# A fused RWKV-style block on Trainium2: two pairs of mixes packed four wide on TensorE, with a new order of the step and PSUM banks from a table

## The reference

```python
xn = _ln(x, ln1_w, ln1_b)
sx = _token_shift(xn, state[:, i1])
xxx = jnp.tanh((xn + sx * maa_x) @ maa_w1).reshape(b, l, 5, 1, EXTRA_MAA)      # 5 x 32
xxx = jnp.matmul(xxx, maa_w2).reshape(b, l, 5, E)                              # five mixes, each 32 -> 512
x5 = xn[:, :, None] + sx[:, :, None] * (maa_stack + xxx)
w = jnp.exp(-jnp.exp(time_decay + jnp.tanh(x5[:, :, 1] @ decay_w1) @ decay_w2))
r = x5[:, :, 3] @ Wr.T;  k = x5[:, :, 0] @ Wk.T;  v = x5[:, :, 2] @ Wv.T       # by heads
g = jax.nn.silu(x5[:, :, 4] @ Wg.T)
def step(s, rkvw):
    a = k_t[:, :, :, None] * v_t[:, :, None, :]
    out = jnp.einsum('bhk,bhkd->bhd', r_t, u * a + s)
    return (a + w_t[:, :, :, None] * s, out)
att = group_norm_over_heads(outs) * gn_w + gn_b
x = x + att * g @ Wo.T
xn2 = _ln(x, ln2_w, ln2_b);  sx2 = _token_shift(xn2, state[:, i0])
rr = jax.nn.sigmoid((xn2 + sx2 * ffn_maa_r) @ ffn_Wr.T)
kk = jnp.square(jax.nn.relu((xn2 + sx2 * ffn_maa_k) @ ffn_Wk.T))
return x + rr * (kk @ ffn_Wv.T)
```

## Time and profile before

| | |
|---|---|
| median of 3 runs | 1659.32 us (1658.87 to 1660.46) |
| the profiled execution | 1657.67 us, its span 1655.9 us |
| TensorE matmul busy | 1590.0 us, 96% of the span, 19990 records |
| VectorE busy | 997.2 us, 60% |
| ScalarE busy | 513.0 us, 31% |
| GpSimd busy | 624.3 us, 38% |
| DMA, mean | 41 GB/s; SyncE's queue 12.2% of 16 engines |
| mean granted TensorE clock | 0.989 |

### The profile page before, as it was taken

How to read it: one execution, slowest core, us unless ns; L and a number is a source line. 1 busy time by engine, 2 the same in 40 slices (tenths; PEclk the granted TensorE clock), 3 DMA queues, 4 the chain that set the end, 5 groups by cost and what they waited for, 6 DMA issues and landing times.

```text
span 1655.9 us, 46091 instructions
## 1 busy us (share of the span) xinstructions
PE 1590.0 (96%) x19990; PEld 1200.0 (72%) x19990; DVE 997.2 (60%) x1990; ACT 513.0 (31%) x910; POOL 624.3 (38%) x512
## 2 busy tenths in 40 slices
PE   8989799999999999999999999999999999999988
PEld 7877577777767777776777777677776767777554
DVE  3263765667666566756657675665767557564642
ACT  1123222323232232423233232323333233332331
POOL 3242532535243253524425252442525235252411
PEclk9999799999999999999999999999999999999999
DMA  7010101102010110201001010110101011010200
GB/s 276 1 37 25 50 23 35 48 7 64 22 62 22 34 50 7 65 22 61 23 21 51 18 64 22 45 39 20 50 20 62 24 35 48 9 49 21 69 11 25
DMA packets 56425, 67.73 MB, mean 41 GB/s; under 512 B 23264, under 2 KB 40032, under 8 KB 55200
## 3 DMA queue, kind: packets, MB, share of 16 engines
q1 hardware_dynamic: 56224, 64.79, 12.2%
HBM read 43.75 MB, written 8.39 MB: 31 GB/s over the span
## 4 chain that ended last, share of the span: by engine, by line
PE 78%; DVE 14%; ACT 4%; POOL 2%; issue 2%; SPq 0%; DMA 0%; ACTq 0%; POOLq 0%; DVEq 0%
PE pair L1116 28%; PE pair L1124 19%; PE pair L1170 4%; PE at_ps L1050 4%; PE at_ps L1043 3%; PE pair L1194 2%; PE kv_ps L1072 2%; DVE kT L590 2%; PE att_ps L1107 2%; PE pair L1132 2%; PE pair L1196 2%; DVE x L679 2%; POOL cen L482 2%; PE pair L1150 2%; DVE gT L709 1%
## 5 line engine op out<-in xcount | busy, mean ns | idle before, releaser
L1116 PE MATMUL pair<-x,wts 128*128 128x256 f32 x2048 | 459.1, 382 | 14.7 <-ACT kT L864 14.3
L1116 PEld LDWEIGHTS pair<-x,wts 128*128 128x128 f32 x2048 | 383.8, 190 | 76.2 <-ACT kT L864 17.0
L456 POOL TENSOR_TENSOR x<-x,xnT 128x1024 f32<-128x1024 f32 x80 | 178.6, 2233 | 218.1 <-DVE x L679 217.4
L679 DVE SCALAR_TENSOR_TENSOR x<-pair,vecs,sx 128x256 f32<-128x256 f32 x320 | 132.4, 475 | 117.1 <-PE pair L1170 116.7
L873 ACT ACTIVATE at<-at_ps 128x512 f32<-128x512 f32 x128 | 76.3, 596 | 184.1 <-PE at_ps L1050 183.9
L1124 PE MATMUL pair<-wts,cen 128*128 128x512 f32 x240 | 110.8, 604 | 0.0
L1050 PE MATMUL at_ps<-rm,kc 128*16 128x128 f32 (+1 forms) x2048 | 110.8, 276 | 0.0
L1124 PE MATMUL pair<-wts,yT 128*128 128x512 f32 x240 | 109.6, 599 | 0.3 <-POOL yT L494 0.3
L1116 PE MATMUL pair<-yT,wts 128*128 128x256 f32 x480 | 107.8, 382 | 0.0
L1124 PE MATMUL pair<-wts,sx 128*128 128x512 f32 x240 | 107.0, 599 | 0.7 <-ACT cen L859 0.7
L1116 PEld LDWEIGHTS pair<-yT,wts 128*128 128x128 f32 x480 | 89.9, 190 | 14.4 <-issue 2.8
(11 more groups left out here) (194 smaller groups left out, 2760.2 us busy)
## 6 DMA issues: line engine op xcount, KB each, us to landing
rm<-rst SPq DMA_DIRECT2D x1024, 12.0 KB
xu<-in_x SPq DMA_DIRECT2D x16, 512.0 KB, 3.7
wts<-in_wts SPq DMA_DIRECT2D x8, 1024.0 KB, 14.6
kvs<-in_s SPq DMA_DIRECT2D x32, 256.0 KB, 3.3
s<-in_s SPq DMA_DIRECT2D x32, 256.0 KB, 2.9
x<-in_x SPq DMA_DIRECT2D x15, 512.0 KB
out<-sx SPq DMA_DIRECT2D x15, 512.0 KB, 3.6
prev<-in_prev SPq DMA_DIRECT2D x32, 4.0 KB, 3.2
```

What stands on the lines that cost most here:

```text
L456: gp.tensor_tensor(t, t, xnT[:, :, :, 1:L1].rearrange("p g b t -> p (g b) t"), ALU.add).then_inc(x5_ready, 1)
L679: last = ve.scalar_tensor_tensor(seqs(x5[q], g), ps[:, :, g * L:(g + 1) * L], vecs[:, vec, g:g + 1], seqs(sx, g), ALU.add, ALU.mult)
L1116: last = pe.matmul(ps[:, g // 2, TB * (g % 2):TB * (g % 2 + 1)], wts[:, m, k, g * P:(g + 1) * P], source[:, k, :], start=(k == 0), stop=(k ...
```

## The change

The mixes are done in three goes. **mixWV** does the mixes W and V together, and **mixKR** K and R: for each channel group and sequence the products of the two mixes follow each other, so that four products in a row lie on four different groups of 32 rows and go to four different PSUM banks. mixG stays alone. The order of the step is rewritten on every engine but SyncE: v is computed first, its two halves around z and decay, then mixKR, k, mixG, r, and g last, behind wo. c02_1 and c1v_1 of the running block move ahead of z. Banks come from a table (`BANK`, and `BANK_FIRST` for step -1) instead of the parity, and `x5_ready` counts in the order V, W, K, R, G. Step -1 gets lists of its own (the `-1` entry of `PE_EDGE` and its like), and `IDLE` is rewritten.

```diff
-MIXES = {"mixW": (MW, 1, 0, 0), "mixK": (MK, 0, 1, 1), "mixG": (MG, 2, 0, 2),
-         "mixR": (MR, 3, 1, 3), "mixV": (MV, 2, 0, 4)}
+MIXES = {"mixV": (MV, 2, 1, 0), "mixW": (MW, 1, 0, 1), "mixK": (MK, 0, 0, 2), "mixR": (MR, 3, 1, 3),
+         "mixG": (MG, 2, 0, 4)}
+JOINT = {"mixWV": ("mixW", "mixV"), "mixKR": ("mixK", "mixR")}
-DENSE = {"k": (WK, 1, 1), "g": (WG, 0, 2), "r": (WR, 1, 3), "v": (WV, 0, 4)}
+DENSE = {"k": (WK, 0, 2), "g": (WG, 0, 4), "r": (WR, 1, 3), "v": (WV, 1, 0)}
...
+BANK = {"mixW": 0, "mixV": 1, "wv": 1, "c02_1": 0, "c1v_1": 1, "z": 0, "v": 1, "decay": 0, "mixK": 0, "mixR": 1,
+        "yT": 0, "k": 1, "mixG": 0, "r": 1, "wo": 0, "g": 1, "x2T": 0, "xT": 1, "c02_0": 0, "kk": 1, "c1v_0": 0,
+        "rr": 1, "h": 0}
+TASKS = list(BANK)
...
-DVE_ORDER = ["mixW", "kv0", "attb1", "chain1", "gn_sum", "wv", "gn_var", "mixK", "c02_1", "gn_rec", "mixG",
+DVE_ORDER = ["mixV", "kv0", "attb1", "mixW", "chain1", "gn_sum", "wv", "c02_1", "c1v_1", "gn_var", "chain1b", "gn_rec",
...
+DVE_EDGE = {-1: ["mixV", "mixW", "mixK", "mixR", "ln1_stats", "ln1", "mixG", "chain0", "xT", "c02_0", "chain0b",
+                 "c1v_0", "g"],
...
+            def joint_mix(names, i, at_):
+
+                a = at_.plus(1)
+                for name in names:
+                    for semaphore, value in readers_before(name, i, at_):
+                        pe.wait_ge(semaphore, value)
+                if i == -1 and names[0] == "mixW":
+                    pe.wait_ge(lora_in, 16 * 8)
+                pe.wait_ge(h_ready, a.count(1, 1))
+                for g in range(G):
+                    for b in range(NB):
+                        for name in names:
+                            lo = MAA * ((MIXES[name][1] + 2 * b) % 4)
+                            last = pe.matmul(bank(name, i)[:, b, g * L:(g + 1) * L],
+                                             maa2[b][lo:lo + MAA, g * P:(g + 1) * P],
+                                             h1[lo:lo + MAA, b * L:(b + 1) * L], start=True, stop=True)
+                            if g == G - 1 and b == NB - 1:
+                                last.then_inc(done[name], 1)
```

More of the change, by code:

```diff
@@ L74 @@
         "ln2", "x2T", "kk", "rr", "wv")
-PE_LAST = {LAST: ["kt0", "V7", "kv0", "wv.0", "aT1", "A0", "wv.1", "V0", "A1", "c02_1", "V1", "c1v_1", "A2", "V2",
+PE_EDGE = {-1: ["mixWV", "v.0", "z", "v.1", "mixKR", "decay", "k.0", "k.1", "mixG", "r.0", "r.1", "xT", "c02_0", "g.0",
+                "g.1", "h", "c1v_0"],
+           LAST: ["kt0", "V7", "kv0", "wv.0", "aT1", "A0", "wv.1", "V0", "A1", "c02_1", "V1", "c1v_1", "A2", "V2",
                   "yT", "A3", "V3", "kt1", "wo.0", "kv1", "wo.1", "aT0", "A4", "V4", "yT@0", "A5", "V5", "x2T", "A6", "V6",
@@ L82 @@
             LAST + 1: ["x2T@1", "kk@1", "rr@1"]}
-DVE_LAST = {LAST: ["kv0", "attb1", "chain1", "gn_sum", "wv", "gn_var", "c02_1", "gn_rec", "c1v_1", "chain1b",
+DVE_EDGE = {-1: ["mixV", "mixW", "mixK", "mixR", "ln1_stats", "ln1", "mixG", "chain0", "xT", "c02_0", "chain0b",
+                 "c1v_0", "g"],
+            LAST: ["kv0", "attb1", "chain1", "gn_sum", "wv", "gn_var", "c02_1", "gn_rec", "c1v_1", "chain1b",
                    "attb0", "kv1", "gn_sum@0", "gn_var@0", "gn_rec@0", "wo", "ln2_stats", "ln2", "x2T", "wo@0",
@@ L86 @@
             LAST + 1: ["wo@1", "ln2_stats@1", "ln2@1", "wv", "x2T@1", "wv@0", "wv@1"]}
-POOL_LAST = {LAST: ["gn_sub", "rch1", "wv", "c02_1", "gn_scale", "bon1", "yT", "rch1b", "gn_sub@0", "gn_scale@0",
+POOL_EDGE = {-1: ["mixV", "mixW", "mixK", "mixR", "ln1_stats", "mixG", "rch0", "c02_0", "rch0b", "bon0"],
+             LAST: ["gn_sub", "rch1", "wv", "c02_1", "gn_scale", "bon1", "yT", "rch1b", "gn_sub@0", "gn_scale@0",
                     "ln2_stats", "yT@0", "ln2_stats@0", "gn_sub@1", "gn_scale@1", "yT@1"],
@@ L91 @@
            LAST + 1: ["out", "out@0", "out@1"]}
-IDLE = {(-2, "xT"): 14, (-2, "h"): 27, (-1, "mixW"): 3, (-1, "z"): 17, (-1, "mixG"): 6, (-1, "k.0"): 3, (-1, "g.0"): 4,
-        (-1, "mixR"): 10, (-1, "mixV"): 6, (-1, "r.0"): 4, (-1, "v.0"): 4, (-1, "c1v_0"): 5, (-1, "h"): 12, (0, "mixW"): 3,
-        (0, "kt0"): 5, (0, "A0"): 14, (0, "V0"): 18}
+IDLE = {(-2, "xT"): 14, (-2, "h"): 27, (-1, "mixWV"): 3, (-1, "v.0"): 14, (-1, "mixKR"): 4, (-1, "decay"): 6,
+        (-1, "k.0"): 4, (-1, "c02_0"): 10, (-1, "c1v_0"): 2, (0, "mixWV"): 2, (0, "kv0"): 2, (0, "A0"): 12}
 class Block:
@@ L830, in step @@
             def step(i, at_):
[L831 removed]
+                for name in DVE_EDGE.get(i, DVE_ORDER if i < LAST else []):
                     if "@" in name:
@@ L1156, in stage @@
                                              ut[:, k, b * L:(b + 1) * L], start=(k == 0), stop=(k == G - 1))
-                elif name in MIXES:
-                    m = MIXES[name][1]
-                    if i == -1 and name == "mixW":
-                        pe.wait_ge(lora_in, 16 * 8)
+                elif name == "mixG":
                     pe.wait_ge(h_ready, a.count(1, 1))
```

56 lines of the change are left out of this document (30 added, 26 removed), and 3 rows, old and new, of the table PE_ORDER.

## The result

The changed kernel takes **1645.24 us** (median of 4 runs, 1644.55 to 1647.49), and the kernel before, run beside it on the same chip, 1659.09 (1658.65 to 1660.46). The ratio is 0.9917, 95% interval 0.99 to 0.9935: faster, by 13.9 us. 1631 was forecast. The time lies inside the range of 1619 to 1652, but the gain is half of the one worked out, 13.9 instead of 28.3 us, so half of the sum needs explaining.

What follows compares the result with a forecast made beforehand. TensorE's own work bounds full steps, a cross-engine chain the start. -1.10 us over thirteen steps (-14.3) and -14.0 at the start give -28.3 on 1657.67, so 1629.4; median 1631, range 1619 to 1652.

Steps and rivals of the forecast that it cites:

- The mixes: TensorE's two joint mixes a step: 32 records at 34 ns take 1.09 us instead of 2.18, so -2.18 us a step.
- The first and second rival: Joint mixes: first, packing under fourfold, 1.4 us each, 1641 (0.22); second, four groups no faster than two, 2.18, 1666 (0.08).
- Waits that go: TensorE's three recurring full-step waits, before g (0.98), mixR (0.34) and c02_1 (0.30), vanish: -1.62 us a step.
- V next to A: V products directly behind their A wait for ScalarE's copy: V1, V2, V3, V6 take 1.15 us, V0 0.87; +0.92 a step.
- New waits: TensorE waits in full steps before k.0 (0.73), xT (0.7) and rr.0 (0.35): +1.78 us a step.
- Covered, I think: Other full-step places, among them kv0, wv, chain1, yT, wo, x2T, c02_0 and h, were expected to bring no new wait.
- The third rival: VectorE, behind a late chain1b, reaches mixK late, so k.0 starts 1.2 us later: +16, 1647 us; chance 0.10.
- The start: Up to step 1: chain0b 14.9 us earlier, V0 at 91, then about 67 us to the next mix; -14.0 us.
- the fourth rival: The start gains only half, because the clock falls or a weight load holds v: 1638 us; chance 0.10.
- Steps 15, 16: 0: The last two steps were forecast to neither gain nor lose time.
- its own two terms of 7: Low end of the range: joints at 0.87 us (-7) and one of the three new waits not coming (-7).

Runs made afterwards that it cites:

- The run with mixW first: Changed kernel with mixW ahead of kv0 and attb1 in VectorE's order: 1638.90 us, ratio 0.9876.
- the run with dummies: Changed kernel with dummy products added on TensorE, 16 before V0 and 7 before k.0 of step 0, 28 before V0 of step 1: 1640.47 us.
- the second run of the changed kernel: The changed kernel run again with nothing altered, beside three of the other runs: 1645.91 us, ratio 0.9909.

## Why the prediction was half right

- **"The mixes", -2.18 a step: the size was right, the reason wrong.** Joints last 1.10 us as forecast (1.09). But a record does not cost half as much on twice as many groups as a law of its own. A block costs 0.2 us and then 112 ns for each record of its fullest group. The prediction had 110 ns at hand, from the dense product, and used it only as the lower bound of 27 ns a record, without the fixed 0.2; with it the bound of 0.87 becomes 1.08. That the forecast came out is luck: all three blocks that I compared have 8 records in a group. The first and second rival fall with that: no 1.4 and no 2.18.
- **"Waits that go", -1.62: right.** None of the three is left.
- **"V next to A", +0.92: right.** V1, V2, V3 and V6 last 1.15, V0 0.87.
- **"New waits", +1.78: right.** 0.79, 0.72 and 0.25, together 1.76.
- **"Covered, I think": this is the step that failed in the full step.** It said of chain1 that mixW's multiplication goes into what was idle time. On VectorE it does. But GpSimd's add of mixW then falls on chain1's first instructions, which take 2.62 us for 1.14, so VectorE's wv, which frees c1v_1's tile, comes later, c1v_1 waits 0.30, and c02_1 and c1v_1 also run 0.3 longer around that wait. The run with mixW first gave 0.56 us a step back. The rest was priced at nothing as well: v cut in two around decay costs 0.2 over one in one piece by the run on it (0.3 by the 7.0 that I took). These make some 0.8 of the 0.84 us that the step is short of the forecast, 13 steps, 11 us.
- **The third rival** (VectorE late to mixK) named the right engine at the wrong place. chain1b took 8.9 us instead of 10.2 and mixK found VectorE free for 3.9.
- **"The start", -14.0: -10.7 at the first mix of step 1.** The laid-out chain was right: chain0b begins at 68.10 (68.8 forecast), V0 at 90.08 (91). What failed is the 1 us that it allowed for the clock: by the run with dummies it was 5.8, and 4.7 against the second run of the changed kernel. TensorE idled 3.89 us ahead of V0, 1.80 ahead of k and 2.22 ahead of h, and what followed ran at 0.56 to 0.62 of the full clock. This is the fourth rival, at half of its size. The number of dummies was in the diff, and I had said that those that go cost nothing in themselves.
- **"Steps 15, 16: 0", and step 14 as a full step: +1.2 for the three.** Step 14 has no xT, so in the new order only V5 stands between x2T and c02_0, and c02_0 waits 1.39 us for ScalarE's copy of x2T (1505.44), where the kernel before waited 0.34. The other part is not steady: V0 of step 15 waits 2.29 us instead of 1.15, but 1.72 in the second run of the changed kernel, 0.83 in the run with dummies and 1.13 in the one with v whole. GpSimd's add is not its cause, as chain1's first four take 1.14 us in step 15; what is stays open.

Sum: 10.9 from the full step, 3.3 from the start, 1.2 from the end, about the 15.6 us by which the gain of the span, 12.7, is short of 28.3 (that of the medians, 13.9, is 14.4 short). The low end of the range, by its own two terms of 7, would be 1617, not 1619.

## What to carry to other kernels

When a step is moved, price what its last stage does to the engine next door, not only the stage on the engine that waits: here an add on GpSimd, hidden in every view of TensorE, took half of the forecast gain of a full step back. Price packing by the records of the fullest group of rows plus a fixed part, and test the rule with twice the records, not with other groups alone. A new order also shows where the waits are thinly covered; four moves of one or two list entries gave 2.7 us a step, more than twice what the change itself was forecast to give there.
